# The last tile's exponentials turned on TensorE as whole fp32, with the fp16 parts made from PSUM

## The reference

```python
# x: 32 x 256 rows of 128 (8192 tokens), fp32
q = x @ Wq.T + bq
scores = q @ memory_keys.T / sqrt(128)              # 4096 keys
probs = softmax(scores)
mem_out = probs @ memory_values
x = layernorm(x + mem_out @ Wo.T + bo)
h = silu((x @ w1.T) * s1) * ((x @ w2.T) * s2)       # 128 -> 512
h = gelu((h @ h1.T) * s_h1)                         # 512 -> 512
h = gelu((h @ h2.T) * s_h2)                         # 512 -> 512
out = layernorm(x + (h @ w3.T) * s3)                # 512 -> 128
```

## Time and profile before

| | |
|---|---|
| median of 3 runs | 1117.41 us (1116.58 to 1117.55) |
| profiled execution, its own time | 1117.46 us |
| span of that execution's instructions | 1115.5 us |
| mean granted TensorE clock | 0.996 of full |
| PE busy | 1079.3 us (97%) |
| DVE, ACT, POOL busy | 972.2, 903.1, 643.0 us |
| last score matmul of frame 31 starts | 723.46 us |
| h1 of block 0 starts on PE | 760.32 us |

### The profile page before, as it was taken

How to read it: one execution, slowest core, us unless ns; L and a number is a source line. 1 busy time by engine, 2 the same in 40 slices (tenths; PEclk the granted TensorE clock), 3 DMA queues, 4 the chain that set the end, 5 groups by cost and what they waited for, 6 DMA issues and landing times.

```text
span 1115.5 us, 20017 instructions
## 1 busy us (share of the span) xinstructions
PE 1079.3 (97%) x5324; PEld 770.6 (69%) x5324; DVE 972.2 (87%) x1806; ACT 903.1 (81%) x1609; POOL 643.0 (58%) x617
## 2 busy tenths in 40 slices
PE   6899999999999999999999999979999999999996
PEld 5666666666666666666666666646888888888875
DVE  6999999999999999999999899897888887888884
ACT  6787788878887888888878878788788888888883
POOL 0487888888888888888888888760211211121111
PEclk9999999999999999999999999999999999999998
DMA  6879888988988889888888998891010010011000
GB/s 202 203 185 212 198 201 210 209 200 202 209 203 206 203 207 210 200 202 209 206 203 204 212 200 188 193 255 55 12 46 28 28 56 28 28 35 50 11 13 27
DMA packets 83957, 165.89 MB, mean 149 GB/s; under 512 B 19664, under 2 KB 47824, under 8 KB 83792
## 3 DMA queue, kind: packets, MB, share of 16 engines
q1 hardware_dynamic: 71536, 154.29, 58.7%
q10 hardware_dynamic: 12384, 11.16, 3.5%
HBM read 22.76 MB, written 8.39 MB: 28 GB/s over the span
## 4 chain that ended last, share of the span: by engine, by line
PE 42%; SPq 13%; issue 11%; POOL 10%; ACT 10%; DMA 6%; DVE 5%; ACTq 1%; POOLq 0%; DVEq 0%
PE ring L1090 13%; SPq L380 12%; PE ring L1091 12%; POOL pT L549 10%; DMA slot_p<-rows 6%; ACT rows L629 5%; ACT pT L638 4%; PE o_ps L1017 2%; PE s_ps L1045 2%; PE s_ps L1043 2%; PE s_ps L1044 2%; PE o_ps L1020 2%; PE o_ps L1022 2%; DVE rows L795 2%; DVE rows L828 1%
## 5 line engine op out<-in xcount | busy, mean ns | idle before, releaser
L549 POOL TENSOR_TENSOR pT<-slot_p,pT 128x512 f16<-128x512 f32 x482 | 546.0, 1167 | 124.4 <-ACT pT L638 124.3
L638 ACT ACTIVATE pT<-slot_p 128x512 f16<-128x512 f32 x512 | 296.5, 617 | 73.8 <-DMA slot_p<-rows 68.6
L828 DVE TENSOR_SCALAR_CACHE_REDUCE rows<-s_ps 128x1024 f32<-128x1024 f32 x256 | 309.4, 1209 | 40.5 <-DMA slot_p<-rows 19.9
L795 DVE STREAM_TRANSPOSE rows<-rows 128x1024 f32<-128x1024 f32 x256 | 316.9, 1239 | 5.9 <-issue 4.1
L629 ACT ACTIVATE rows<-rows,bias 128x1024 f32<-128x1024 f32 x256 | 291.6, 1139 | 6.4 <-DVE bias L836 5.9
L1043 PE MATMUL s_ps<-keys,q_buf 128*128 128x512 f32 x512 | 249.2, 487 | 6.8 <-DVE rows L828 3.5
L1017 PE MATMUL o_ps<-pT,v_hi 128*128 128x512 f16 x512 | 197.4, 385 | 13.3 <-POOL pT L549 6.6
L1045 PE MATMUL s_ps<-keys,q_buf 128*128 128x512 f32 x512 | 202.4, 395 | 0.0
L1044 PE MATMUL s_ps<-keys,q_buf 128*128 128x512 f32 x512 | 201.1, 393 | 0.0
L1020 PE MATMUL o_ps<-pT,v_lo 128*128 128x256 f16 x1024 | 196.1, 273 | 0.0
L1022 PE MATMUL o_ps<-pT,v_hi 128*128 128x512 f16 x512 | 194.6, 380 | 0.0
(11 more groups left out here) (110 smaller groups left out, 1329.2 us busy)
## 6 DMA issues: line engine op xcount, KB each, us to landing
slot_p<-rows SPq DMA_DIRECT2D x1024, 128.0 KB, 3.0
x_in<-in_x SPq DMA_DIRECT2D x16, 256.0 KB, 3.4
x_in<-in_xT ACTq DMA_DIRECT2D x30, 128.0 KB, 3.3
out<-y_out SPq DMA_DIRECT2D x15, 256.0 KB, 2.4
o_scratch<-o_sum ACTq DMA_DIRECT2D x29, 128.0 KB, 2.7
o_in<-o_scratch SPq DMA_DIRECT2D x14, 256.0 KB, 3.1
z<-in_w_all ACTq DMA_DIRECT2D x25, 113.0 KB, 2.7
rows<-in_w_all SPq DMA_DIRECT2D x1, 2816.0 KB, 12.1
```

The source lines that it names most:

```text
L549: nc.gpsimd.tensor_tensor(halves(s % RING, 1), slots_first(pp, s), halves(s % RING, 0), ALU.subtract).then_inc(split, 1)
L638: nc.scalar.activation(halves(s % RING, 0), slots_first(pp, s), ACT.Copy).then_inc(highed, 1)
L795: nc.vector.transpose(row_piece(tile, k), row_piece(tile, k)).then_inc(turned, 1)
L828: nc.vector.tensor_scalar(row_piece(tile, k), s_ps[:, j % 2, :], 1.0, None, ALU.mult, ALU.max, accum_out=part_max[:, tile, k:k + 1]).then_ ...
```

## The change

For the last tile (pair 31, tile 1) alone, DVE's four turns and SP's 16 DMAs are left out. PE turns the exponentials with full 128 x 128 fp32 transposes, four at a time into one PSUM bank (`turn_unit`); such a unit is two steps, and there are eight. Two banks, `y_ps` and `x1_ps`, take turns. ACT makes the unit's high part for tile 0 from `slot_p` and for tile 1 from PSUM (`unit_high`, two instructions of 128 x 512), POOL makes the low part of tile 0 and DVE that of tile 1, with the PSUM bank as one input. So that a transpose of neighbouring slots gives the order that the values have, the score matmuls of this tile read the keys with a stride (`by_chunk`).

Around it: of pair 30's low parts DVE now makes steps 7, 8, 9, 11, 13 and 15, POOL the rest. ACT spreads the four exponentials over the high parts of pair 30 (behind steps 4, 6, 8 and 10) and takes `keep_x1T(0)` behind step 10. DVE does `split_x1(0)` behind its step 9. PE runs `turn_unit(0)` and `turn_unit(1)` behind step 10 of pair 30, and each further unit's transposes ahead of the values of the unit two before it; the second half of the first layer comes behind unit 2, and `turn_x1(1)` behind all values. The moments of block 1 move behind DVE's unit 1, its reciprocal deviation behind POOL's unit 2, its normalisation behind DVE's unit 6. The form for weights with low parts becomes one whole-fp32 matmul a product, so the raw weights are loaded by two DMAs (one behind the last scores, one behind all values) in place of one, and POOL no longer reads `low_max` or branches. Products of block 0 get four places in `rows` in place of two. Two waits of ACT in the turns (`mid1_done`, `used_by`) stand one instruction earlier. Buffers in SBUF are placed anew.

```diff
-LATE_STEP = 12
+LOW_BY_DVE = (7, 8, 9, 11, 13, 15)
+LOW_BY_POOL = tuple(s for s in range(STEPS) if s not in LOW_BY_DVE)
+UNITS = STEPS // 2
...
+    def unit_part(u, tile, low):
+        return pT[:, 2 * u % RING:2 * u % RING + 2, :, (2 * low + tile) * P:(2 * low + tile + 1) * P].rearrange(
+            "p s c (a t) -> p (s c) a t", t=G)
+    def unit_slots(u):
+        return slot_p[:, 1, 0:GROUPS, 4 * u:4 * u + 4, :].rearrange("p a c t -> p c a t")
+    def unit_bank(u):
+        return stage.y_ps[:, :, :] if u % 2 == 0 else stage.x1_ps[:, :].rearrange("p (s d) -> p s d", d=P)
+    def unit_turned(u):
+        return unit_bank(u).rearrange("p s (a t) -> p s a t", t=G)
...
 (SP)
-        for k in range(PIECES):
-            exchange(PAIRS - 1, 1, 1, k)
...
-        sp.dma_start(raw, w_raw[:, 0:W_COLS]).then_inc(raw_loaded, 16)
+        sp.wait_ge(scored, 8 * PAIRS)
+        sp.dma_start(raw_in, w_raw[:, 0:W_AT["h1"]]).then_inc(raw_loaded[0], 16)
         stage.store_output(sp, PAIRS - 2)
         stage.store_output(sp, PAIRS - 1)
+        sp.wait_ge(pv_done, 16 * PAIRS)
+        sp.dma_start(raw_rest, w_raw[:, W_AT["h1"]:W_COLS]).then_inc(raw_loaded[1], 16)
...
 (POOL)
-        for s in range(STEPS - T_LAG, LATE_STEP):
-            if s == 4:
+        for s in LOW_BY_POOL[STEPS - T_LAG:]:
+            low_part(PAIRS - 2, 0, s)
+        for u in range(UNITS):
+            pool.wait_ge(highed, 16 * (PAIRS - 1) + 2 * u + 1)
+            nc.gpsimd.tensor_tensor(unit_part(u, 0, 1), unit_slots(u), unit_part(u, 0, 0), ALU.subtract).then_inc(split, 1)
+            if u == 2:
                 stage.inverse_deviation(pool, 1, 0)
-            low_part(PAIRS - 2, 0, s)
...
 (ACT)
+        def unit_high(u):
+            if u == 0:
+                for k in range(PIECES):
+                    act.wait_ge(sent[0][k], 16 * GROUPS * PAIRS)
+            act.wait_ge(pv_done, 16 * (PAIRS - 1) + 2 * u + 2 - RING)
+            nc.scalar.activation(unit_part(u, 0, 0), unit_slots(u), ACT.Copy).then_inc(highed, 1)
+            act.wait_ge(unit_made, u + 1)
+            nc.scalar.activation(unit_part(u, 1, 0), unit_turned(u), ACT.Copy).then_inc(highed, 1)
+
+        after_high = {4: 0, 6: 1, 8: 2, 10: 3}
+        for s in range(STEPS - T_LAG, STEPS):
             high_part(PAIRS - 2, 0, s)
-            if s == 6:
+            if s == 3:
+                stage.output_half(act, PAIRS - 3, 1)
+            if s in after_high:
+                exp_piece(PAIRS - 1, 1, after_high[s])
+            if s == 10:
                 act.wait_ge(sent[0][0], 16 * GROUPS * PAIRS)
                 stage.keep_x1T(act, 0)
...
-        stage.output_half(act, PAIRS - 2, 0)
-        for s in range(STEPS):
-            high_part(PAIRS - 1, 1, s)
-            if s == 8:
+        for u in range(UNITS):
+            unit_high(u)
+            if u == 3:
+                stage.output_half(act, PAIRS - 2, 0)
+            if u == 4:
                 gate_of(0, 2)
-            if s == 11:
+            if u == 5:
                 gate_of(0, 3)
-            if s == 13:
+            if u == 6:
                 load_table(ACT.Gelu)
                 product_high(0, 2)
         stage.keep_x1T(act, 1)
         product_high(0, 3)
...
 (DVE)
         turn_piece(PAIRS - 1, 0, PIECES - 1)
-        stage.residual(dve, 1)
-        for k in range(PIECES):
-            turn_piece(PAIRS - 1, 1, k)
+        stage.residual_sum(dve, 1)
         stage.output_sum(dve, PAIRS - 3, 1)
-        stage.split_x1(dve, 0)
-        for s in range(LATE_STEP, STEPS):
+        for s in LOW_BY_DVE:
             low_part(PAIRS - 2, 0, s)
+            if s == 9:
+                stage.split_x1(dve, 0)
...
-        for s in range(STEPS):
-            low_part(PAIRS - 1, 1, s)
+        for u in range(UNITS):
+            dve.wait_ge(highed, 16 * (PAIRS - 1) + 2 * u + 2)
+            nc.vector.tensor_tensor(unit_part(u, 1, 1), unit_turned(u), unit_part(u, 1, 0), ALU.subtract).then_inc(split_last, 1)
+            if u == 1:
+                dve.wait_ge(stage.z1_ready, 8)
+                stage.moments_of(dve, 1, 0, stage.z1)
...
 (PE)
+        def by_chunk(keys_part, c):
+            return keys_part.rearrange("p (k c t) -> p c k t", k=GROUPS, t=G)[:, 4 * c:4 * c + 4, :, :]
...
+        def turn_unit(u):
+            if u < 2:
+                pe.wait_ge(exped, 8 * PAIRS)
+                pe.wait_ge(*((stage.z1_ready, 8) if u == 0 else (stage.x1T_ready, 1)))
+            else:
+                pe.wait_ge(split_last, len(LOW_BY_DVE) + u - 1)
+            for n in range(4):
+                last = nc.tensor.transpose(unit_bank(u)[:, n, :], rows[:, SLOTS + (4 * u + n) * P:SLOTS + (4 * u + n + 1) * P], stage.ident[:, :])
+            last.then_inc(unit_made, 1)
...
                     first_layer(0, (0, 1), low_weights)
-            first_layer(0, (2, 3), low_weights)
+                if s == 10:
+                    turn_unit(0)
+                    turn_unit(1)
+            for u in range(UNITS):
+                if u + 2 < UNITS:
+                    turn_unit(u + 2)
+                add_values(PAIRS - 1, 1, 2 * u)
+                add_values(PAIRS - 1, 1, 2 * u + 1)
+                if u == 2:
+                    first_layer(0, (2, 3), low_weights)
             stage.turn_x1(pe, 1)
-            for s in range(STEPS):
-                add_values(PAIRS - 1, 1, s)
```

More of the change, by code:

```diff
@@ L94, with __init__ @@
 class RowStage:
-    def __init__(self, nc, ctx, x_rows, o_dram, o_stored, den, keys, rows):
+    def __init__(self, nc, ctx, x_rows, o_dram, o_stored, den, rows):
         def sb(name, shape, dt):
@@ L252, in store_output, with layers @@
         sp.dma_start(self.o_dram[:, bass.ds(p * 2 * P, 2 * P)], self.o_sum[:, :]).then_inc(self.o_stored, 16)
-def layers(nc, stage, hold, xT, wqT, bq, kT, vT, woT, bo, scale_cols, w_raw, den, keys, rows, out_rows):
+def layers(nc, stage, hold, xT, wqT, bq, kT, vT, woT, bo, scale_cols, w_raw, den, rows, out_rows):
     def sem(name):
@@ L386, in layers @@
     w_hi = stage.w_all[:, 0:W_COLS]
[L387 to L390, removed]
+    stage.x1_hi, stage.x1_lo = (sb(name, [P, BT], FP32R)[:, :] for name in ("x1_hi", "x1_lo"))
+    in_room = sb("in_room", [P, 2, HC, BT], FP32R)[:, :, :, :]
+    raw_in = sb("raw_in", [P, W_AT["h1"]], FP32)[:, :]
+    sb("key_room", [P, 2 * SLOTS - 2 * BT - 2 * HC * BT - W_AT["h1"]], FP32)
+    raw_rest = sb("raw_rest", [P, W_COLS - W_AT["h1"]], FP32)[:, :]
     x1T, x1_hi, x1_lo, scales, table_room = stage.x1T, stage.x1_hi, stage.x1_lo, stage.scales, stage.table_room
@@ L1081, in _, with split_products, whole_products, layer @@
         frames(pe, frame)
-        def split_products(out, pairs, sem_done, low_weights, parts_ready=None):
-            for n, (wh, wl, hh, hl) in enumerate(pairs):
+        def split_products(out, pairs, sem_done, parts_ready=None):
+            for n, (w, hh, hl) in enumerate(pairs):
                 if parts_ready:
                     pe.wait_ge(parts_ready[0], parts_ready[1] + n + 1)
-                final = n == len(pairs) - 1
-                nc.tensor.matmul(out, wh, hh, start=n == 0, stop=False)
-                last = nc.tensor.matmul(out, wh, hl, start=False, stop=final and not low_weights)
-                if low_weights:
-                    last = nc.tensor.matmul(out, wl, hh, start=False, stop=final)
-            last.then_inc(sem_done, 1)
-        def layer(out, name, j, src, sem_done, low_weights, width=HID, parts_ready=None):
-            split_products(out, [(weight(name, k, j, width), weight_low(name, k, j, width),
-                                  h_hi[src][:, k, :], h_lo[src][:, k, :]) for k in range(HC)], sem_done, low_weights,
-                           parts_ready if j == 0 else None)
+                nc.tensor.matmul(out, w, hh, start=n == 0, stop=False)
+                last = nc.tensor.matmul(out, w, hl, start=False, stop=n == len(pairs) - 1)
+            last.then_inc(sem_done, 1)
+        def whole_products(out, pairs, sem_done, parts_ready=None):
+            for n, (w, h) in enumerate(pairs):
+                if parts_ready:
+                    pe.wait_ge(parts_ready[0], parts_ready[1] + n + 1)
+                last = nc.tensor.matmul(out, w, h, start=n == 0, stop=n == len(pairs) - 1)
+            last.then_inc(sem_done, 1)
+        def layer(out, b, name, j, src, sem_done, low_weights, width=HID, parts_ready=None):
+            parts_ready = parts_ready if j == 0 else None
+            if low_weights:
+                whole_products(out, [(raw_weight(name, k, j, width), gelu[:, src - 1, k, :] if src else product(b, k))
+                                     for k in range(HC)], sem_done, parts_ready)
+            else:
+                split_products(out, [(weight(name, k, j, width), h_hi[src][:, k, :], h_lo[src][:, k, :])
+                                     for k in range(HC)], sem_done, parts_ready)
         def bank_read_by_in(b, bank):
```

92 lines of the change are left out of this document (39 added, 53 removed).

## The result

The changed kernel takes 1120.72 us (median of 8 runs, 1118.77 to 1121.62) where the kernel before, run beside it, takes 1116.87 (8 runs, 1116.31 to 1117.55). The ratio is 1.0031, with a 95% interval of 1.0022 to 1.0041: slower by 3.5 us (the two medians are 3.85 apart), and above the range that was given. The profiled execution took 1121.62 us, its span is 1119.9.

The account below looks back on a forecast made before the run. PE was taken as the bound from the layers on, paced before them by POOL's low parts. An h1 0.6 us earlier, 0.35 of waiting and 0.3 for semaphores summed to 0: 1117.5 us, range 1115.4 to 1120.0.

Parts of the forecast that it names:

- at no cost: Items priced at nothing: dropped turns and DMAs, raw weights' loads, SP's earlier loads, ACT's two moved waits, POOL's moved `add_bias(2)`.
- a turn of the layers whose length differs from before: In the layers, listed as a sign that the prediction is wrong; no size given.
- The clock: Rival, chance 0.18: PE's clock falls behind the 2.4 us wait at the first layer, costing 1.7 us, to 1119.2.
- The wait is shorter than 3.39: Ahead of the first layer: argument against the clock rival, PE waiting 2.4 us where it stood 3.39 before.
- The wait at h1: Ahead of h1's fourth pair of matmuls: PE waits 0.35 us, as ACT copies `turn_x1(1)` before product copy 3.
- the first layer's start: After pair 30's step 8: starts at 736.5, 2.4 us earlier than before, behind a 2.4 us wait for `split_x1(0)`.
- the transposes: Last tile on PE: four transposes a unit at 0.45 us, 3.6 for eight units; bounds 0.33 and 0.60 a unit.
- ACT's PSUM copy: Unit's high part for tile 1: 0.58 us, taken from `keep_x1T`; bounds 0.52 and 0.62.
- DVE's part of a unit: Low part of tile 1, one PSUM input: near 0.70 us, bounds 0.64 and 0.78, without contending with POOL.
- the stretch from the first layer to h1: PE is the bound: 19.65 us plus 3.6 of transposes, so h1 starts at 759.75, 0.6 earlier.
- semaphores at the new hand-overs: Eight new hand-overs of the last tile's units: 0.3 us added to the sum.
- Strided keys: Rival, chance 0.08: the last tile's 24 score matmuls slow down by up to 5.5 us, to 1122.0.

Follow-up runs that it names:

- the places put back: The changed kernel with keys ahead of `w_all` again and `x1_hi`, `x1_lo` and `in_room` as parts of them, as before: 1118.83 us, ratio 1.0015.
- the new places alone: The kernel before with only the changed kernel's placement (keys behind the stage's tiles, own tiles for the three buffers): 1120.29 us, ratio 1.0021.
- filling the wait: The changed kernel with ten fp32r matmuls of 128x512, result read by nobody, on PE ahead of the first layer: 1119.53 us, ratio 1.0019.
- with 64 B: The changed kernel with one unused buffer of 64 B a partition ahead of all layers' buffers: 1114.05 us, ratio 0.9972.

## Why the prediction was wrong

**The failed step** is a term that the working left out, the new places of the buffers. Under "at no cost" it weighed the turns, the loads and the waits, but not that `x1_hi`, `x1_lo` and `in_room` get new addresses. The section on the change says that the buffers are placed anew, and this term was put at nothing without a reason. The runs put 2.0 us there in the profile (286.34 against 284.36 for 13 turns) and 1.8 and 2.3 by the times (the places put back: 1.0031 to 1.0015; the new places alone: 1.0021). This is what puts the time outside the range: with the places put back the kernel takes 1118.83, inside the 1115.4 to 1120.0. The trace of the kernel before had a hint, which the prediction didn't read: in one turn the products over `keys` come 0.2265 apart and those over `h_hi` 0.2335. The sentence "a turn of the layers whose length differs from before", among the signs of being wrong, came true.

**The clock** was the rival at 0.18, and it came true: with the right place (behind the wait of 2.4), about the right size (1.7 forecast, 1.7 read from the windows, 1.5 between the traces with and without it, 1.3 by the ratios from filling the wait), and too low a chance. The eight times of the changed kernel support that it isn't in all of them: the three with a mean clock of 0.998 have a mean of 1119.5, the five with 0.995 and 0.996 have 1121.1. In the kernel before the fall came where PE also waited for POOL's parts (0.85 and 0.90 us busy from 735 to 737 in the earlier trace rows). That it cost little there, and that taking POOL's waits away uncovered it, is argued and not measured. "The wait is shorter than 3.39" did not keep it away: it fell in the three profiles with 3.39, in two of the six with 2.40 to 2.42, and in one of the two with 1.94 and 1.97. Whether the length counts, so few can't tell.

The Trainium skill (TensorE: Matmul & The Clock Gate, Part 4), by which transposes don't count as busy, was not tested: the clock was up again at 741.9, before the first unit at 742.08, and later units stand among fp16 steps.

**The wait at h1** was there for the reason given, and mis-sized: forecast 0.35, measured 0.69 in starts (0.92 less 0.23) and 0.80 when taken away.

**Right were** the first layer's start, 13.04 us behind the last score matmul in the forecast (736.5 from 723.46) and in the trace (737.20 from 724.16), on the 2.42 us wait for `split_x1(0)` (that the two agree to 0.01 is chance: five other profiles with the same order up to there have 13.5 to 14.1); the transposes, 0.44 a unit for 0.45; ACT's PSUM copy, 0.58 for 0.58; DVE's part of a unit at 0.69 and POOL's at 1.16, side by side at 759.32 and 758.88 (the Trainium skill, SBUF — State Buffer, "Who interferes with whom": by that rule, no lock between them with one SBUF input; the trace agrees); and the stretch from the first layer to h1. Forecast at 23.25, it is 24.60 in the changed kernel, of which 1.5 to 1.7 is the clock, and 23.1 in the trace of the filled wait, where the clock stayed up. The 0.3 us that the sum had for semaphores at the new hand-overs doesn't show there. Strided keys cost nothing that shows: the scores of the last tile come 0.23 to 0.24 apart.

The sum by what was measured in the two profiles: places 2.1 (1.98 in the turns, and an estimate of 0.14 for block 0's h1, 24 matmuls at 0.006 more), clock 1.5 (24.60 less 23.1), the wait at h1 0.75 (the rest of 0.89), and the earlier h1 without the clock's fall -0.7 (-2.39 and 23.1 - 21.43). That is 3.65, for 3.5 by the ratio of the times. It adds up because it is read from one pair of traces; in three of the eight executions the clock's term seems to be missing. In the two profiled spans the frames add another 0.7 ahead of the change's place.

## What to carry to other kernels

A diff that moves a buffer has a term for it: before the next change is weighed, list which tiles get new addresses, and read the start-to-start time of the matmuls over each. If same-shaped fp32r matmuls of one kernel run at two paces, try the moving tile and the weights a multiple of 256 B apart. Here it took one line and gave more than the change cost, though nothing for the score matmuls. And where the clock falls while PE waits for a slow engine, a change that takes those waits away can lay the fall on full work: fill PE's wait, or price the fall in the forecast and not among the rivals.

## What the runs showed that was not expected

The time from start to start of a 128x512 fp32r matmul hangs on the distance between weights and moving tile modulo 256 B in long runs of them: 0.227 us at 0, 0.230 at 64, 0.232 to 0.235 at the other multiples of 32. The score matmuls, six at a time, don't follow it. Other dtypes, other widths and distances that are no multiple of 32 B were not run, nor what in the chip causes it. A PE that stands for 1.94 to 2.42 us in one piece loses its upper clock in some executions and keeps it in others, with the same wait: the changed kernel stood for 2.42 and lost it, with 64 B it stood for 2.41 and kept it. What decides between them stays open.
